# A fused cross-attention and FFN block in fp32 on one core: all words of the hand-written order are dealt out anew, and VectorE waits for its own output in one more place

## The reference

```
x = x + tanh(g0) * (softmax(q k^T / 4) v @ wo + bo)     # 16 heads of 16; q from layernorm(x), k and v from the context
x = x + tanh(g1) * ffn(layernorm(x))
ffn(y): probs = softmax(y @ router_w); top 2 of 8, divided by their sum; their total w (one number per token)
        out = (gelu(y @ w1 + b1) @ w2 + b2) * w
```

## Time and profile before

| | |
|---|---|
| median of 3 runs | 709.57 us (709.5 to 710.0) |
| the profiled execution, first to last instruction | 1105.9 us; what lies around the span is not shown |
| mean granted TensorE clock in it | 0.556 of 2.4 GHz |
| PE busy | 1088.8 us, 98% |
| DVE, ACT, POOL busy | 526.6, 408.3, 329.7 us |
| DMA queue q1 | 26.4% of 16 engines' span |

### The profile page before, as it was taken

How to read it: one execution, slowest core, us unless ns; L and a number is a source line. 1 busy time by engine, 2 the same in 40 slices (tenths; PEclk the granted TensorE clock), 3 DMA queues, 4 the chain that set the end, 5 groups by cost and what they waited for, 6 DMA issues and landing times.

```text
span 1105.9 us, 20672 instructions
## 1 busy us (share of the span) xinstructions
PE 1088.8 (98%) x7648; PEld 972.5 (88%) x7648; DVE 526.6 (48%) x1299; ACT 408.3 (37%) x797; POOL 329.7 (30%) x474
## 2 busy tenths in 40 slices
PE   5999999999999999999999999999999999999998
PEld 5787988989899898998989889898998989988888
DVE  5764554545445454454544545455454544544422
ACT  2243443423334243342433334234343333424332
POOL 3733521322323242241422404223132332212241
PEclk7555555555555555555555555555555555555555
DMA  6645231222312123131231403324122231200000
GB/s 189 187 124 140 78 99 31 74 69 74 99 52 71 52 74 99 52 95 28 74 98 52 117 14 83 82 64 110 42 61 70 74 99 52 63 24 10 2 10 17
DMA packets 47797, 80.27 MB, mean 73 GB/s; under 512 B 10997, under 2 KB 30802, under 8 KB 47698
## 3 DMA queue, kind: packets, MB, share of 16 engines
q1 hardware_dynamic: 47378, 78.18, 26.4%
q10 hardware_dynamic: 320, 0.77, 0.3%
HBM read 30.49 MB, written 11.01 MB: 38 GB/s over the span
## 4 chain that ended last, share of the span: by engine, by line
PE 97%; SPq 1%; DVE 1%; DMA 0%; POOL 0%; issue 0%; ACT 0%; POOLq 0%
PE P L951 48%; PE S L980 13%; PE OT L1010 12%; PE T L992 12%; PE P L1036 4%; PE TR L1019 2%; PE TR L1095 2%; PE TR L1026 1%; PE TR L1078 1%; PE TR L1063 1%; SPq L430 1%; PE TR L966 1%; DMA CTRAW<-in_ctxT 0%; DVE NEGM L783 0%; POOL CT_LO L591 0%
## 5 line engine op out<-in xcount | busy, mean ns | idle before, releaser
L783 DVE TENSOR_REDUCE NEGM<-S 112x1 f32<-112x375 f32 x512 | 272.3, 542 | 186.5 <-PE S L980 181.9
L703 ACT ACTIVATE PROBS<-T 125x448 f32<-125x448 f32 x384 | 204.2, 543 | 208.1 <-PE T L992 199.7
L980 PE MATMUL S<-KS,QS 96*112 96x376 f32 x512 | 239.6, 484 | 1.7 <-DVE NEGM L783 1.7
L992 PE MATMUL T<-QS,KS 98*125 98x224 f32 x768 | 209.1, 376 | 0.0
L992 PEld LDWEIGHTS T<-QS,KS 98*125 98x125 f32 x768 | 169.6, 244 | 22.9 <-issue 7.1
L1010 PE MATMUL OT<-PROBS,VA 125*17 125x112 f32 x3072 | 140.1, 364 | 0.0
L980 PEld LDWEIGHTS S<-KS,QS 96*112 96x112 f32 x512 | 118.3, 239 | 19.1 <-issue 10.2
L1010 PEld LDWEIGHTS OT<-PROBS,VA 125*17 125x17 f32 x3072 | 107.4, 128 | 21.0 <-issue 9.3
L606 POOL CAST HT_HI<-HG 128x224 fp32r<-128x224 f32 x124 | 45.9, 370 | 256.5 <-ACT HG L729 255.1
L729 ACT ACTIVATE HG<-P,B 128x224 f32<-128x224 f32 x128 | 57.3, 447 | 123.2 <-PE P L951 123.2
L951 PE MATMUL P<-W_HI,HT_LO 128*112 128x256 f32 x256 | 98.9, 386 | 0.0
(11 more groups left out here) (112 smaller groups left out, 1817.5 us busy)
## 6 DMA issues: line engine op xcount, KB each, us to landing
KS<-KHI SPq DMA_DIRECT2D x124, 188.0 KB, 3.0
KS<-KLO SPq DMA_DIRECT2D x128, 94.0 KB, 2.7
CTRAW<-in_ctxT SPq DMA_DIRECT2D x32, 375.0 KB, 3.3
QS<-q_parts SPq DMA_DIRECT2D x96, 112.0 KB, 3.1
X<-in_x SPq DMA_DIRECT2D x16, 224.0 KB, 3.6
q_parts<-QHI SPq DMA_DIRECT2D x32, 112.0 KB, 2.3
q_parts<-QLO SPq DMA_DIRECT2D x32, 112.0 KB, 2.3
out_y<-X SPq DMA_DIRECT2D x16, 224.0 KB, 3.5
```

The lines of the kernel that those rows point to most:

```text
L703: act.activation(PT[0:KN, k, pp * 4 * SQ:(pp + 1) * 4 * SQ], T_BANK[i % 2][0:KN, 0:4 * SQ], ACT.Exp, scale=SCALE).then_inc(exp_done, 1)
L783: dve.tensor_reduce(NEGM[:, b.par, col:col + 1], S_BANK[i % 2][0:SQ, 0:SK], AX.X, ALU.max, negate=True).then_inc(max_done, 1)
L980: pe.matmul(S_BANK[i % 2][0:SQ, 0:SKP], QS[0:96, b.gpar, i % 2, i // 2, b.j * SQ:(b.j + 1) * SQ], KS[0:96, b.ring, i // 2, :], start=True, ...
L992: mm = pe.matmul(T_BANK[i % 2][0:KN, r * 2 * SQ:(r + 1) * 2 * SQ], KS[0:98, prv.ring, pair, k * KN:(k + 1) * KN], QS[0:98, prv.gpar, :, pa ...
```

## The change

The lists of words are replaced. The same stages are issued the same number of times, on the same engines with the same shapes; only their order differs. The text of the lists is also laid out in another way (the steady pair of steps stands in the first list, with one word left in the second; most of the fill in the lists of steps -3 and 3, most of the drain in 32 and 35), which by itself has no effect. The first line of the steady order and the only other edit are:

```
 ORDER = [stages(text) for text in (
-    """st.5+1 dh.0+2 s.11+1 n2+1 dn.0+2 st.6+1 wo+1 x2n+2 st.7+1 s.12+1 st.8+1 dh.1+2 st.9+1 dn.1+2 kd.0+1
+    """n1+1 s.8+1 kd.0+1 st.2+1 l1 st.3+1 dh.0+2 s.9+1 st.4+1 st.5+1 n2+1 dn.0+2 st.6+1 s.10+1 st.7+1 wo+1 x2n+2
...
                             if past(pg.group(GB)):
                                 dve.wait_ge(x1b_done, pg.group(GB))
+                                dve.wait_ge(y_done, pg.group(GB))
                             dve.tensor_scalar(WT[:, :], WS[:, :], TG[0:SQ, 1:2], None, ALU.mult).then_inc(wt_done, 1)
```

More of the change, by code:

```diff
@@ L71 @@
 ORDER = [stages(text) for text in (
[L72 to L76, removed]
@@ L77 @@
-    """mt st.7+1 s.1 st.8+1 s.2 k.0 st.9+1 st.10+1 s.3 k.1 st.11+1 pv.0+1 pv.1+1 pv.2+1 l1-1 pv.3+1 m s.4
-       au+1 rw.7+1 s.5 st.0 v.0 n2+1 s.6 st.1 s.7 v.1 st.2 st.3 s.8 s.9 n1 wo+1 st.4 s.10 qs+1 lo.7+1 xb+2""")]
-SPECIAL = {k: stages(text) for k, text in (
[L82 to L101, removed]
-       st.11+1 kd.0+1 kd.1+1 cl+1 pv.1+1 pv.2+1 pv.3+1 s.4 au+1 v.2+1 s.5 st.0 st.1 s.6 v.0 m s.7 st.2 s.8
-       st.3 rw.4+1 wo+1 st.4 qs+1 n1 rw.5+1 rw.6+1 s.9 xb+2 v.1 rw.7+1 s.10"""),
-    (32, """st.5+1 s.11+1 n2+1 pv.0+1 st.6+1 s.12+1 st.7+1 s.13+1 wo+1 s.14+1 st.8+1 st.9+1 s.15+1 x2n+2 dh.0+2
-       mt pv.1+1 pv.2+1 x2t st.10+1 st.11+1 dn.0+2 rt st.0 st.1 rx dh.1+2 st.2 rw.0 rw.1 rw.2 rw.3 st.3 au+1
-       rw.4 pv.3+1 st.4 st.5 dn.1+2 st.6 rw.5 st.7 pv.0 rw.6 rw.7 lo.0 st.8 st.9 pv.1 st.10 st.11 n1 up.0
-       lo.1 up.1 m pv.2 ol+1 lo.2 pv.3 n2"""),
-    (33, """au+1 up.2+1 lo.3+1 up.3+1 lo.4+1 n1 up.4+1 lo.5+1 wo+1 n2 up.5+1 wo up.6+1 up.7+1 x2n+1 dh.0+1 ol
[L109 to L112, removed]
@@ new lines @@
+    """n1+1 s.8+1 kd.0+1 st.2+1 l1 st.3+1 dh.0+2 s.9+1 st.4+1 st.5+1 n2+1 dn.0+2 st.6+1 s.10+1 st.7+1 wo+1 x2n+2
+       st.8+1 st.9+1 s.11+1 dh.1+2 k.0 dn.1+2 s.12+1 s.13+1 x2t st.10+1 st.11+1 v.1+1 s.14+1 s.15+1 lo.0 k.1 rt
+       s.0 xn rx kd.1+1 up.0 mt pv.0+1 pv.1+1 rw.0 lo.1 pv.2+1 lo.2 pv.3+1 ql+1 xl s.1 rw.1 up.1 s.2 up.2 s.3
+       up.3 s.4 lo.3 au+1 up.4 s.5 rw.2 s.6 m up.5 up.6 s.7 s.8 up.7 s.9 n1 st.0 lo.4 st.1 s.10 s.11 v.2+1 s.12
+       xt ol+1 st.2 rw.3 v.0 s.13 st.3 s.14 q.0 xb+1 st.4 s.15 kd.1 st.5 q.1 s.0-1 cl+1 st.6 kd.0 s.1-1 mt-1
+       k.0-1 st.7 s.2-1 k.1-1 st.8 s.3-1 st.9 v.1 st.10 v.2 rw.4 ct lo.5 s.4-1 qs s.5-1 lo.6 st.11 pv.0 pv.1 m-1
+       pv.2 pv.3 n2 s.6-1 cl rw.5 st.0-1 lo.7 rw.6 s.7-1 ct-1 st.1-1 v.0-1 rw.7 wo""",
```

38 lines of the change are left out of this document (added).

## The result

| | before | changed |
|---|---|---|
| runs, median us | 709.79 (709.50 to 711.58, 4 runs) | 720.19 (718.71 to 721.49, 4 runs) |
| profiled execution: time, span, clock | 709.73, 707.7, 0.995 | 719.68, 717.6, 0.990 |

The ratio is 1.0099 with a 95% interval of 1.0051 to 1.0146: the change is slower by 10.4 us, 1.0%. The forecast was 707.4 us, a gain, and the range 695 to 719 us; the measured time lies 1.2 us above the range.

What follows compares the result with a forecast made beforehand. The prediction took PE to run at the upper clock with some 104 us of waits, about 5 us a pair outside fill and drain. Its terms summed to -2.2 us, giving 707.4 us; range 695 to 719 us.

Steps and rivals of the forecast that it cites:

- bound by PE: Rival for the whole run: PE at a mixed clock, about 0.87, sets the time; 709.6 +- 1 us, within a 0.22 chance.
- Terms 1 to 5: Steady pairs: gelu buffer ring -5.2, `wo` to `x2t` -2.6, `rt` to `mt` +3.9, VectorE's stretch +2.6, ScalarE's stretch -1.3 us.
- Term 3: PE's `mt` behind `rt` waits until LG is read: 0.6 us missing a pair, half counted, loss 3.9 us.
- Term 6: VectorE's added wait for L930 of the pair before, some 26 us earlier in its own order: cost 0.
- Term 7: Fill: first product about 1.0 us later, three more products ahead of the first `s`; net gain 0.8 us.
- Term 8: Drain: the last `x2t` has 2.2 us of PE behind the last `wo` and needs 3.4; loss 1.2 us.
- Table loads: Two more in the fill at 1.28 us each; by the skill, a switch costs about 2.66 us with the flush.
- `mt` decides: Rival: PE's `mt` behind `rt` waits for LG with nothing absorbed, 718.6 us; chance 0.31 with others like it.

Runs made afterwards that it cites:

- before profiled again: The unchanged kernel, profiled a second time, now at the clock of the timed runs (the first trace ran near half clock): 709.73 us.
- all3: The changed kernel with before's start, three products put back among the first scores, and the last six FFN weight loads earlier: 748.43 us, ratio 1.0509.
- fill_new_no_loads: Before's order with the change's for steps -3 to 5 and the added wait, without the loads of the last five FFN weight parts: 716.53 us, ratio 1.0043.
- weights: The changed kernel with the loads of the last six FFN weight parts moved earlier in SP's queue: 746.33 us, ratio 1.0483.

## Why the prediction was wrong, point by point

**What bounds the kernel: the step that failed.** "The rest, some 5 us for each pair, is waits in the steady part." The sum behind it was 1088.8 x 0.556 = 605 us of PE at the upper level. PE is busy 685.8 us in before profiled again, at a clock of 0.995. PE's time did not shrink with the clock: a pair went from 67.5 us to 41.55, a factor of 0.616 where 0.556 was used. The rival "bound by PE" was right about the steady part and wrong about why: not a mixed clock of 0.87, but more time at the full one. The columns that I counted were too cheap as well: start to start in that pair, a score takes 0.19 us where I had 0.16, an `up` 0.66 for 0.56, a `dh` or `dn` 1.43 for 1.28. The observation that the runs agree within 0.5 us could not tell these apart, and it rested on three runs: the 107 of before beside the experiments lie between 709.35 and 719.54 us.

**Terms 1 to 5** (net -3.2 us: -5.2, -2.6, +3.9, +2.6, -1.3). From 115 to 600 us PE waits in neither kernel. The places exist, and a full PE hides all of them. Term 3's, in the change, VectorE and then PE:

```profile
308.27 0.61 DVE L799 SCALAR_TENSOR_TENSOR KLO<-P,BK,KHI 128x376 fp32r<-128x376 f32 x1 [0.65 <-ACT KHI L687]
308.79 0.18 DVE L874 TENSOR_REDUCE LG<-TR 112x16 f32<-112x32 f32 x1
```
```profile
309.08 0.26 PE L975 MATMUL TR<-IDENT,NEGM 112*16 112x112 f32 x1
```

`k.1` ended on PE at 307.46 us. LG was done 1.51 us later (I had 1.7), and PE's work up to `mt` took 1.62 us (I had 1.12: the router's products alone take 0.71). So `mt` did not wait, by 0.11 us. What the steady order does change was in no term: 0.27 us of PE a pair. By the starts in PE's timeline it sits in the neighbours of instructions: eight products with WO take 1.54 us a pair instead of 1.35 (transposes of AU stand between them), the 32 scores 6.24 instead of 6.06, and all others together 0.08 us less. Why a neighbour costs that was not tried.

**Term 6**, the added wait: 0, as measured.

**Term 7**, the fill: forecast a gain of 0.8 (bounds -3.5 and +3), measured a loss of 6.6 to 7.6 us. "First product about 1.0 us later" was 2.0 in the trace of the change, but that is scatter: with the change's start it came at 7.1 to 7.6 us in eight profiles and at 8.4 to 8.5 in three (6.5 to 6.6 in most with before's), so the 1.0 was about right. What failed first is "three more products stand ahead of the first `s`": it is no gain, since `s` waits for the q parts, as the text itself said, and these came later: the first score stood at 32.09 us, and at 31.1 in the mean of seven profiles with the change's start, where the text had put it at 30.5 at most. But the larger part, 4.0 us, was in no term. I had looked at the loads of the first 30 us and at two table loads, and never followed `lw` and `w` past them. The fourth `lw` is issued at 69.11 us where it was at 58.46, and from there each load leaves only when the split before it is done. Following each queue of a step that is moved would have found it in the order: `lw.3` behind `w.3` and two K copies.

**Term 8**, the drain: forecast 1.2 us, and PE did wait 1.1 us for XN ahead of its last such transposes. But before's two waits of scores for NEGM there, 1.4 us together, are 0.7 in the change. By the two traces the drain's net is 0. Over all profiles the new drain is the steadier one: 99.5 to 99.6 us in ten of eleven (100.3 in the other), where before's took 99.7 to 99.8 in four of eight, 101.2 to 101.3 in three and 103.6 in one (the profile of the earlier trace rows left out).

**Table loads.** By the Trainium skill (ScalarE: Activation LUTs, What ACT_TABLE_LOAD costs) a flush follows a load. Here none is seen: the load of 98.43 us took 1.28, and the gelu behind it started at 99.72.

**The rival `mt` decides** gave 718.6 us, close to the measured 720.2, by a mechanism that did not occur. That is a coincidence.

**What stays open.** The start of the fill, 3.2 us in the two traces: the first transpose of NEGM came at 43.3 to 46.2 us in seven profiles with the change's start untouched (mean 44.6) and at 41.9 to 45.3 in five with before's (mean 43.1). So some 1.4 us of the 3.2 are the start's, and the rest is scatter from one execution to the next. The clock has a part in the scatter: of the seven, the four whose clock had risen again by 39.6 us took 13.0 to 13.1 us from the first score to the first transpose, the three that were at 0.50 until after 41.4 us took 14.0 to 14.1 (the change among them), with the same words on PE. Why the first score is 1.8 us later in the mean (31.1, and 29.3 with before's start) stays open: the order of the first loads was only tried behind the blockade of all3. What makes the median of fill_new_no_loads 4.8 us longer than before's is open too.

## What to carry to other kernels

A trace taken at another clock than the timed runs gives durations but no waits, and PE's time must not be scaled by the clock ratio: profile again until the execution resembles the runs, and only then say what bounds the kernel. In a loop that keeps PE full, the order of a list moved only 0.27 us a pair here and the fill 7.6 us, so cost fill and drain first, with every load chain followed to its end. A queue that issues in order turns a load that is placed too early into a blockade of everything behind it (weights took 26 us more than the change), and one placed too late into a wait of whoever consumes it.
